# A graph-attention layer's edges in groups of 2048 instead of tiles of 1024, with SyncE's order of loads and stores changed

## The chip, the core and the metric

One core of a Trainium2 chip runs the kernel. The time is device microseconds (us) of one execution. It was taken three times: 4876.2, 4891.12 and 4896.5 us, median 4891.12. One more execution was profiled; it took 4895.69 us.

## The reference, cut to what matters

12,500 nodes with 64 features, 400,000 edges, sorted by their target node dst. All is float32.

```python
h_src, h_dst = nfeats[src], nfeats[dst]
e = leaky_relu(concat([h_src, h_dst, efeats]) @ W_attn + b_attn, 0.01)[:, 0]   # one score an edge
m = concat([h_src, efeats]) @ W_ne                                             # one message an edge
emax = segment_max(e, dst)
ex = exp(e - emax[dst])
z = segment_sum((ex / segment_sum(ex, dst)[dst])[:, None] * m, dst)
out = relu(concat([nfeats, z]) @ W_out)
x = layernorm(nfeats + out)
```

## The kernel before

The edges go through in 391 tiles of 1024 (`ST`), eight on each of 128 partitions. A tile's features lie in one of ten slots of `V` (`RING`): the 64 edge features, loaded by SyncE (`load_ef`), and the 64 features of the source nodes, gathered by POOL with eight indirect DMAs of 128 rows (`gather`, L365). A slot is filled anew when PE has counted up its `v_free` (L902).

Since the edges are sorted, the targets of a tile lie close together. A *window* is 128 consecutive nodes that begin at the tile's first target, one on each partition; they cut through two blocks of 128 nodes, b and b+1, and `half` says which of the two a partition's node is in. Each engine runs an inner loop over the tile's windows (`Fori(0, windows)`), whose number it loads from `trip`. With this input every tile has one window, 391 in all.

What happens in window G, by engine:

- DVE, for the tile two ahead: the product of `V` with the attention weights `wa` (L621) and its sum for each edge, the scores `u` (L625). SyncE stores them to DRAM (L259) and loads them back spread over all partitions as `ubc` (L264), and the tile's targets likewise as `dbc` (L254).
- ACT: `psS`, a huge number wherever an edge's target is not the partition's node, 0 where it is (L498, a Square of `dbc` with a bias).
- DVE: `um` = `ubc` - `psS` and, in the same instruction, its maximum for each node (L735, the *masked maximum*; L735 also stands for the small read of the result). From it and the node's own score come the running bounds (L739, L741) and the new node state (L743).
- ACT: `alpha`, the factor by which older sums must shrink (L502, L505), and the two exponentials `zs` and `zb` of the two branches of the leaky ReLU (L507, L508).
- DVE: `e1` = the greater of both (L694, `weigh`); this is done at the start of the next window.
- PE: transposes `e1` in eight pieces to `psT` (L855), in two halves of four. ACT copies each half to `pT` (L460, `weights_out`). PE multiplies the pieces with `V` into `psG` (L861), each in two passes.
- ACT scales the accumulator rows by `alpha` (L470, `rescale`), and DVE adds `psG` to them (L687, `merge`).

The exponentials, transposes, matmuls and merging of one tile are spread over the following windows: `LAG` = 3 windows lie between a window and its merging, and `psG` has two banks. SyncE's order for each tile is (`step`, L300): wait for the scores and store them, load dst, load the spread scores, load the source indices three tiles ahead (`AHEAD`), wait for the free slot, load the edge features. The loops are written out over ten tiles, one turn of the ring. In the first 70 tiles 49 pairs of node blocks are also transposed and multiplied on the side (`x_pair`, `y_pair`). After the last tile come the division, the second matrix product, the layer norm and the output.

## Time and profile before

| what | value |
|---|---|
| times of three executions | 4876.2, 4891.12, 4896.5 us |
| profiled execution, its time | 4895.69 us |
| its span, first to last instruction | 4893.9 us |
| busy: PE, DVE, ACT, POOL | 2096.0, 2615.8, 2270.5, 3429.4 us |
| granted TensorE clock, mean | 0.650 of full |
| queue q1 (SyncE's loads and stores) | 519.51 MB, 35.5% of the 16 DMA engines' time |
| queue q0 (POOL's gathers) | 102.60 MB, 12.6% |

Busy is the time in which an engine executes; waiting and an engine's own sequencing are not in it. "idle before" is the gap between an instruction and the one before it on its engine, and the name behind it is what ended that gap: "issue" means that nothing in the profile explains it, "remote" that something outside this core's instructions did, often a DMA. A letter q behind an engine's name is its sequencer. The matmuls' ends are modelled.

### The profile page before, as it was taken

To read this page: it belongs to the slowest core of one execution; us is meant where nothing else is said; L and a number is where in the kernel's file an instruction comes from. 1 tells how busy PE (TensorE), PEld (TensorE's weight loads), DVE (VectorE), ACT (ScalarE), POOL (GpSimd) and SP (SyncE) were. 2 spreads that over 40 slices of the span, in tenths; PEclk is the share of its full clock that TensorE was granted. 3 is DMA by queue.
4 is the path that set the end of the run, shared out by engine and by line. 5 is a ranking of instruction groups with operands and counts; after the bars stand their busy time and mean duration, and the time that the engine had idled before them with its cause. 6 is when DMAs were issued, how large, how long until landed. Compare 5 with 4: busy or idle time off the path is not lost.

```text
span 4893.9 us, 64908 instructions
## 1 busy us (share of the span) xinstructions
PE 2096.0 (43%) x10260; PEld 1948.9 (40%) x10261; DVE 2615.8 (53%) x4868; ACT 2270.5 (46%) x4123; POOL 3429.4 (70%) x3149
## 2 busy tenths in 40 slices
PE   0444444444444344443444444444444444444446
PEld 0434444433334334343433433343333334443436
DVE  5545555554555455554555555555545555555557
ACT  1545555544444444444444444444444445444444
POOL 6677776777777667777777767777677777777751
PEclk8666666666666666666666666666666666666666
DMA  5445444554555445444445444554444544544541
GB/s 113 129 124 142 123 132 128 136 132 129 130 133 137 119 130 134 133 134 130 130 132 139 130 122 127 137 134 130 132 128 130 141 130 129 130 130 131 137 124 52
DMA packets 759572, 628.94 MB, mean 129 GB/s; under 512 B 608412, under 2 KB 608796, under 8 KB 759332
## 3 DMA queue, kind: packets, MB, share of 16 engines
q1 hardware_dynamic: 646164, 519.51, 35.5%
q0 software_dynamic: 100096, 102.60, 12.6%
q10 hardware_dynamic: 13072, 4.80, 0.5%
q14 instruction: 233, 1.91, 0.1%
q8 instruction: 7, 0.11, 0.0%
HBM read 621.58 MB, written 4.81 MB: 128 GB/s over the span
## 4 chain that ended last, share of the span: by engine, by line
issue 27%; another core or an unknown queue 23%; DVE 20%; DVEq 13%; ACT 11%; ACTq 5%; PE 2%; POOL 0%
DVE u L625 5%; DVE e L694 5%; DVEq L749 3%; DVE prod L621 3%; ACT psS L498 2%; DVE acc L687 2%; ACT zs L507 2%; DVEq L716 2%; ACT zb L508 2%; ACTq L512 2%; ACT acc L470 1%; ACT pT L460 1%; DVEq L687 1%; DVE bounds L739 1%
## 5 line engine op out<-in xcount | busy, mean ns | idle before, releaser
L365 POOL DMA_INDIRECT V<-in_x_dram,srcs x3128 | 3404.1, 1088 | 1343.3 <-issue 907.5
L855 PE MATMUL psT<-ident,e 128*128 128x128 f32 x3136 | 824.4, 414 | 2739.2 <-DVE e L694 1642.7
L855 PEld LDWEIGHTS psT<-ident,e 128*128 128x128 f32 x3136 | 599.5, 217 | 2882.1 <-DVE e L694 1726.6
L861 PE MATMUL psG<-V,pT 128*128 x6288 | 1364.1, 390 | 0.0
L861 PEld LDWEIGHTS psG<-V,pT 128*128 128x128 f32 x6288 | 1314.5, 307 | 0.0
L460 ACT COPY pT<-psT 128x512 f32<-128x512 f32 x785 | 451.8, 576 | 1372.7 <-remote 1316.1
L621 DVE TENSOR_TENSOR prod<-V,wa 128x1024 f32<-128x1024 f32 x391 | 479.5, 1226 | 563.3 <-issue 563.2
L694 DVE TENSOR_TENSOR e<-zb,zs 128x1024 f32<-128x1024 f32 x392 | 480.4, 1226 | 491.2 <-remote 427.3
L735 DVE CUSTOM_DVE_ANT_0 um<-ubc,psS 128x1024 f32<-128x1024 f32 x391 | 477.3, 1221 | 129.8 <-ACT psS L498 99.3
L625 DVE TENSOR_REDUCE u<-prod 128x8 f32<-128x1024 f32 x391 | 477.0, 1220 | 51.1 <-issue 18.2
L508 ACT ACTIVATE zb<-um,ebias 128x1024 f32<-128x1024 f32 x391 | 442.9, 1133 | 0.0
L498 ACT ACTIVATE psS<-dbc,nbias 128x1024 f32<-128x1024 int32 x391 | 436.9, 1118 | 12.7
L507 ACT ACTIVATE zs<-um,ebias 128x1024 f32<-128x1024 f32 x391 | 442.8, 1132 | 0.0
L502 ACT ACTIVATE ebias<-wnode,nn 128x3 f32<-128x3 f32 x391 | 115.3, 295 | 703.2 <-DVE nn L741 455.0
L687 DVE SCALAR_TENSOR_TENSOR acc<-psG,half,acc x788 | 242.5, 348 | 340.2 <-issue 188.9
L726 DVE TENSOR_SCALAR wnode<-node,half 128x3 f32 x391 | 91.2, 233 | 565.1 <-issue 348.6
L470 ACT ACTIVATE acc<-acc,alpha x788 | 273.3, 397 | 1.3 <-DVE acc L687 1.1
L496 ACT ACTIVATE nbias<-nidbias,wshift 128x1 f32 x391 | 114.9, 294 | 121.7 <-issue 120.0
L505 ACT ACTIVATE alpha<-half,ebias x391 | 115.6, 296 | 108.7 <-issue 61.7
L743 DVE SCALAR_TENSOR_TENSOR node<-keep,nn,node (+1 forms) x391 | 87.0, 223 | 73.5 <-DVE nn L741 38.6
L902 PE MATMUL psR<-ident 128*32 128x128 f32 x390 | 122.9, 315 | 0.0
L739 DVE SCALAR_TENSOR_TENSOR bounds<-slopes,cmax,wnode 128x3 f32<-128x3 f32 x391 | 87.0, 223 | 15.1 <-DVE cmax L735 0.5
(96 smaller groups left out, 620.9 us busy)
## 6 DMA issues: line engine op xcount, KB each, us to landing
ubc<-scores SPq DMA_DIRECT2D x391, 512.0 KB
dbc<-in_dst_dram SPq DMA_DIRECT2D x390, 512.0 KB
V<-in_edge_attr_dram SPq DMA_DIRECT2D x390, 256.0 KB
V<-in_x_dram,srcs POOLq DMA_INDIRECT x3128
scores<-u SPq DMA_DIRECT2D x391, 4.0 KB
srcs<-in_src_dram SPq DMA_DIRECT2D x390, 4.0 KB
out_dram<-y SPq DMA_DIRECT2D x12, 256.0 KB
xt<-in_x_dram ACTq DMA_DIRECT2D x6, 448.0 KB
```

Source lines behind the costliest of these rows:

```text
L365: nc.gpsimd.indirect_dma_start(V[0:n, s, j, 0:F], None, x[:, :], bass.IndirectOffsetOnAxis(ap=srcs[0:n, s, j:j + 1], axis=0)).then_inc(h_i ...
L460: nc.scalar.copy(pT[:, i, :], psT[:, i, :]).then_inc(pt[i], 1)
L498: nc.scalar.activation(psS[:, :], dbc[:, s % 2, :], ACT.Square, bias=nbias[:, 0:1], scale=FAR).then_inc(sq_done, 1)
L507: nc.scalar.activation(zs[:, :], um[:, :], ACT.Exp, bias=ebias[:, 1:2], scale=SLOPE)
L508: nc.scalar.activation(zb[:, :], um[:, :], ACT.Exp, bias=ebias[:, 0:1]).then_inc(e_done, 1)
L621: return nc.vector.tensor_tensor(prod[:, :].rearrange("p (j k f) -> p j k f", k=2, f=F), V[:, s, :, 0:2 * F].rearrange("p j (k f) -> p j k ...
L625: return nc.vector.tensor_reduce(u[:, i, :], prod[:, :].rearrange("p (j f) -> p j f", f=2 * F), AX, ALU.add)
L687: last = nc.vector.scalar_tensor_tensor(row, psG[:, bass.ds(bk, 1), 0:AW].rearrange("p a f -> p (a f)"), half[:, bass.ds(tb, 1), i], row, ...
L694: nc.vector.tensor_tensor(e1[:, :], zb[:, :], zs[:, :], ALU.max).then_inc(mx_done, 1)
L735: nc.vector.tensor_tensor_reduce(out=um[:, :], in0=ubc[:, r, :], in1=psS[:, :], scale=1.0, scalar=-3e38, op0=ALU.subtract, op1=ALU.max, ac ...
L855: last = nc.tensor.transpose(psT[:, i, j * P:(j + 1) * P], e1[:, :].rearrange("q (p j) -> q j p", j=J)[:, 4 * i + j, :], ident[:, :])
L861: last = nc.tensor.matmul(psG[:, bass.ds(bk, 1), 0:AW].rearrange("p a f -> p (a f)"), pT[:, i, j * P:(j + 1) * P], V[:, bass.ds(sv, 1), 4 ...
```

## The change

Two consecutive tiles are now one *group* of 2048 edges: 195 groups and a last one with one tile. A window is gone through once for a group. By the input's targets 192 groups have one window and the last four full ones have two, 200 in all.

- There is one `dbc` and one `ubc` place for each half of a group (h = 0, 1), and both halves go through the one `psS` in turn: square and masked maximum of half 0, then of half 1.
- The leaky ReLU is taken before the exponential. ACT writes `SLOPE` * `um` plus a bias to `psS`, DVE puts the greater of this and of `um` plus a bias into `um` (`low_done`, `lr_done`), half by half. Then one exponential for each half gives `e1`. `zb`, `zs` and L694 are gone.
- ACT's order in a window: nbias, square, square, scaled copy, scaled copy, dif, alpha, rescale, two copies of 128x1024 from `psT` to `pT`, two exponentials.
- PE's order in a window: the 16 matmuls of the group before, then the 16 transposes of this one. `psG` has one bank, `LAG` is 2. The slots of the group before are freed by PE's sequencer once those matmuls are done; the small transpose of L902 is gone.
- The weights of the product lie in PSUM (`wa_v` in `psM`). The node pairs share this PSUM tile, and the product waits for them (`y_ready`), and they for it (`prod_done`).
- SyncE adds up the numbers of windows and waits for `um_done[1]`, the second masked maximum of a group's last window; then it loads the next group's two dst and two spread scores. Behind these it stores the scores of the group after that, loads indices two groups ahead and the edge features. `scores` and `u` have four places instead of two.
- The loops of DVE and SyncE are written out over two turns of the ring.

```diff
-LAG = 3
-BEHIND = 2
-AHEAD = 3
+LAG = 2
+AHEAD = 4
...
+        psT = ps("psT", [P, 2, ST])
+        psG = ps("psG", [P, 512])
         psM = ps("psM", [P, 512])
-        wa_v = wa[:, :].rearrange("p (k f) -> p k f", f=F)[:, 0:3:2, :]
-        xT_y = psM[:, 0:P]
-        y_out = psM[:, P:2 * P]
+        wa_v = psM[:, 0:2 * F].rearrange("p (k f) -> p k f", f=F)
+        xT_y = psM[:, P:2 * P]
+        y_out = psM[:, 2 * P:3 * P]
...
+            def group_read(q):
+                count = sp.value_load(trip[0:1, bass.ds(2 * q + 1, 1)], min_val=1, max_val=NB)
+                sp.reg_add(read, read, count)
+                sp.wait_ge(um_done[1], sp.snap(read))
+            def pair(turn, i, q, odd, stored, last):
+                group_read(q - 2)
+                for h in range(2):
+                    load_dst(2 * q - 2 + h, h)
+                    spread_scores(stored, h, 2 - 2 * odd + h)
+                for h in range(2):
+                    store_scores(2 * q + h, 2 * odd + h)
...
+                for h in range(2):
+                    sp.wait_ge(v_free[2 * i + h], turn + (1 if i == RING // 2 - 1 else 0))
+                    load_ef(RING * turn + 2 * i + h, 2 * i + h)
...
                 windows = act.snap(count, min_val=1, max_val=NB)
-                if ahead:
-                    act.wait_ge(d_in[s % 2], 16 * (RING // 2 * k + s // 2) + 16)
-                else:
-                    act.wait_ge(d_in[s % 2], 16 * (t // 2) + 32)
+                act.wait_ge(d_in[0], arrived[0])
+                act.wait_ge(d_in[1], arrived[1])
...
+                    nc.scalar.activation(psS[:, :], dbc[:, 0, :], ACT.Square, bias=nbias[:, 0:1], scale=FAR).then_inc(sq_done[0], 1)
+                    act.wait_ge(um_done[0], G)
+                    nc.scalar.activation(psS[:, :], dbc[:, 1, :], ACT.Square, bias=nbias[:, 0:1], scale=FAR).then_inc(sq_done[1], 1)
+                    act.wait_ge(wn1, G)
+                    act.wait_ge(um_done[1], G)
+                    nc.scalar.activation(psS[:, :], um[:, 0:ST], ACT.Identity, bias=wnode[:, 4:5], scale=SLOPE).then_inc(low_done[0], 1)
+                    act.wait_ge(lr_done[0], G)
+                    nc.scalar.activation(psS[:, :], um[:, ST:DT], ACT.Identity, bias=wnode[:, 4:5], scale=SLOPE).then_inc(low_done[1], 1)
+                    act.wait_ge(nn_done, G)
+                    nc.scalar.activation(dif[:, :], wnode[:, 2:3], ACT.Identity, bias=nn[:, 0:1], scale=-1.0).then_inc(dif_done, 1)
...
+                    nc.scalar.activation(alpha[:, bass.ds(act.snap(slots[0], min_val=0, max_val=LAG), 1), :].rearrange("p a k -> p (a k)"),
+                                         half[:, bass.ds(q, 1), :].rearrange("p a k -> p (a k)"), ACT.Exp, scale=dif[:, 0:1])
+                    rescale(G)
+                    weights_out(G, 0)
                     weights_out(G, 1)
...
-                    act.wait_ge(nn_done, G)
-                    nc.scalar.activation(ebias[:, :], wnode[:, :], ACT.Identity, bias=nn[:, 0:1], scale=-1.0).then_inc(ebias_done, 1)
...
-                    nc.scalar.activation(zs[:, :], um[:, :], ACT.Exp, bias=ebias[:, 1:2], scale=SLOPE)
-                    nc.scalar.activation(zb[:, :], um[:, :], ACT.Exp, bias=ebias[:, 0:1]).then_inc(e_done, 1)
-                    weights_out(G, 0)
+                    for i in range(2):
+                        act.wait_ge(lr_done[i], G)
+                        nc.scalar.activation(e1[:, i * ST:(i + 1) * ST], um[:, i * ST:(i + 1) * ST], ACT.Exp, bias=nn[:, 0:1]).then_inc(e_done[i], 1)
...
-            def weigh(G):
-                dve.wait_ge(e_done, G)
-                dve.wait_ge(tr[1], G)
-                nc.vector.tensor_tensor(e1[:, :], zb[:, :], zs[:, :], ALU.max).then_inc(mx_done, 1)
...
+                dve.wait_ge(ef_in[s], 16 * turn + 16)
+                dve.wait_ge(h_in[s], 16 * J * turn + 16 * J)
+                if y_steps is not None:
+                    dve.wait_ge(y_ready, y_steps + 1)
+                edge_product(s).then_inc(prod_done, 1)
...
+                    dve.wait_ge(u_in[0], 16 * q + 16)
                     dve.wait_ge(node_set, G)
-                    dve.wait_ge(u_in[r], scored)
-                    dve.wait_ge(e_done, G)
+                    dve.wait_ge(e_done[1], G)
...
-                    weigh(G)
+                    dve.wait_ge(lowf_in, 16)
+                    dve.wait_ge(e_done[0], G)
+                    dve.wait_ge(sq_done[0], G)
+                    nc.vector.tensor_tensor_reduce(out=um[:, 0:ST], in0=ubc[:, 0, :], in1=psS[:, :], scale=1.0, scalar=-3e38,
+                                                   op0=ALU.subtract, op1=ALU.max, accum_out=cmax[:, 0:1]).then_inc(um_done[0], 1)
                     dve.wait_ge(wn0, G)
+                    if left >= 1:
+                        dve.wait_ge(u_in[1], 16 * q + 16)
                     nc.vector.scalar_tensor_tensor(wnode[:, :], node[:, bass.ds(b + 1, 1), :].rearrange("p a k -> p (a k)"), half[:, ts, 1], wnode[:, :],
                                                    ALU.mult, ALU.add).then_inc(wn1, 1)
...
+                    dve.wait_ge(acc_cleared, 2)
+                    dve.wait_ge(um_done[0], G)
+                    dve.wait_ge(sq_done[1], G)
+                    nc.vector.tensor_tensor_reduce(out=um[:, ST:DT], in0=ubc[:, 1, :], in1=psS[:, :], scale=1.0, scalar=-3e38,
+                                                   op0=ALU.subtract, op1=ALU.max, accum_out=cmax[:, 1:2]).then_inc(um_done[1], 1)
+                    dve.wait_ge(um_done[1], G)
+                    nc.vector.tensor_tensor(cm[:, :], cmax[:, 0:1], cmax[:, 1:2], ALU.max).then_inc(cm_done, 1)
...
+                    nc.vector.scalar_tensor_tensor(bounds[:, :], slopes[:, :], cm[:, 0:1], wnode[:, 0:3], ALU.mult, ALU.add).then_inc(bounds_done, 1)
...
+                    for h in range(2):
+                        dve.wait_ge(low_done[h], G)
+                        nc.vector.scalar_tensor_tensor(um[:, h * ST:(h + 1) * ST], um[:, h * ST:(h + 1) * ST], wnode[:, 3:4], psS[:, :],
+                                                       ALU.add, ALU.max).then_inc(lr_done[h], 1)
                     merge(G)
                     pass_on()
...
-                    dve.wait_ge(ef_in[s2], 16 * k2 + 16)
-                    dve.wait_ge(h_in[s2], 16 * J * k2 + 16 * J)
-                    edge_product(s2).then_inc(prod_done, 1)
-                    dve.wait_ge(u_out, 16 * t + 16)
-                    dve.wait_ge(prod_done, t + 1)
-                    edge_score(r).then_inc(u_done, 1)
-                    dve.wait_ge(u_done, t + 3)
...
+                sv = pe.snap(slot[1], min_val=0, max_val=RING - 2)
+                pe.wait_ge(pt[0], G)
+                pe.wait_ge(merged, G + 1)
+                multiply(0, sv)
+                pe.wait_ge(pt[1], G)
+                multiply(1, sv)
                 if turns:
-                    pe.wait_ge(mx_done, G)
-                    pe.wait_ge(pt[0], G)
-                    turn(0)
-                if multiplies:
-                    pe.wait_ge(pt[0], G)
-                    pe.wait_ge(merged, G)
-                    multiply(0, sv, bk)
-                pe.wait_ge(pt[1], G)
-                if turns:
-                    turn(1)
-                if multiplies:
-                    multiply(1, sv, bk)
+                    for i in range(2):
+                        pe.wait_ge(e_done[i], G + 1)
+                        turn(i)
...
-                    nc.tensor.transpose(psR[0:32, 0:P], ident[:, 0:32], ident[:, :]).then_inc(v_free[(s - BEHIND) % RING], 1)
-                    pe.load(coming, trip[0:1, bass.ds(2 * t + 3, 1)])
+                    pe.load(coming, trip[0:1, bass.ds(2 * q + 3, 1)])
+                    pe.wait_ge(agg_done, pe.snap(g))
+                    for h in range(2):
+                        pe.sem_inc(v_free[(2 * i - 2 + h) % RING], 1)
```

The instructions of SyncE in the steady state, before: one tile. `trip` holds the numbers of windows, `u_done` counts DVE's sums, `v_free` PE's releases.

```order
L259 DMA scores<-u 128x8 [waits u_done]
L254 DMA dbc<-in_dst_dram 128x1024
L263 ISA
L264 DMA ubc<-scores 128x1024 [waits u_out]
L248 ISA [waits h_in1]
L248 DMA srcs<-in_src_dram 128x8
L251 ISA [waits v_free8]
L251 DMA V<-in_edge_attr_dram 128x8x64
```

And after: one group.

```order
L306 TENSOR_LOAD trip
L306 ISA x2
L307 ISA
L256 DMA dbc<-in_dst_dram 128x1024 [waits um1_done]
L266 DMA ubc<-scores 128x1024 [waits u_out0]
L256 DMA dbc<-in_dst_dram 128x1024
L266 DMA ubc<-scores 128x1024 [waits u_out1]
L261 DMA scores<-u 128x8 [waits u_done] x2
L250 DMA srcs<-in_src_dram 128x8 [waits h_in4]
L250 DMA srcs<-in_src_dram 128x8 [waits h_in5]
L253 DMA V<-in_edge_attr_dram 128x8x64 [waits v_free0]
L253 DMA V<-in_edge_attr_dram 128x8x64 [waits v_free1]
```

The stores of scores moved from ahead of the loads of dst to behind them; ahead of these stands a load of `trip` and the wait for `um1_done`; the loads of indices and edge features stay last.

ACT before, the second half of a window, from its rescaling of `acc` on; `zs` and `zb` are the exponentials, `tr0` counts the transposes of a first half.

```order
L470 ACTIVATE acc<-acc,alpha 128x129
L502 ACTIVATE ebias<-wnode,nn 128x3 [waits nn_done]
L505 ISA [waits ebias_done,lowf_in]
L505 REGISTER_ALU
L505 ACTIVATE alpha<-half,ebias 128x2
L507 ACTIVATE zs<-um,ebias 128x1024
L508 ACTIVATE zb<-um,ebias 128x1024
L460 COPY pT<-psT 128x512 [waits agg_half,tr0]
```

And after, from the first square of a window on; `um0_done` and `um1_done` count the masked maxima, `lr0_done` the first maximum with the scaled copy.

```order
L525 ACTIVATE psS<-dbc,nbias 128x1024 [waits nbias_done]
L527 ACTIVATE psS<-dbc,nbias 128x1024 [waits um0_done]
L530 ACTIVATE psS<-um,wnode 128x1024 [waits um1_done,wn1]
L532 ACTIVATE psS<-um,wnode 128x1024 [waits lr0_done]
L534 ACTIVATE dif<-wnode,nn 128x1 [waits nn_done]
L537 ISA [waits dif_done,lowf_in]
L537 REGISTER_ALU
L537 ACTIVATE alpha<-half,dif 128x2
L494 ISA
```

Here stand four passes through `psS` in a row (L525 to L532), of which the last three wait for DVE. The rest of that window on ACT, in which `e` is the exponential that PE transposes:

```order
L500 ISA [waits merged,lowf_in]
L500 ACTIVATE acc<-acc,alpha 128x129
L500 ISA
L500 REGISTER_ALU
L500 ACTIVATE acc<-acc,alpha 128x129
L490 COPY pT<-psT 128x1024 [waits agg_half,tr0]
L490 COPY pT<-psT 128x1024 [waits agg_done,tr1]
L544 ACTIVATE e<-um,nn 128x1024 [waits lr0_done]
L544 ACTIVATE e<-um,nn 128x1024 [waits lr1_done]
```

The copies from `psT` to `pT` moved ahead of the exponentials and stand behind the four passes.

## Rows read from the trace of the kernel before

**Rows 1.** The page: the span; queue q1, packets, MB, share; POOL's costliest group.

```profile
span 4893.9 us, 64908 instructions
...
q1 hardware_dynamic: 646164, 519.51, 35.5%
...
L365 POOL DMA_INDIRECT V<-in_x_dram,srcs x3128 | 3404.1, 1088 | 1343.3 <-issue 907.5
```

**Rows 2.** Line L365 alone: ns min/median/max; idle us and times by what ended it.

```profile
L365 POOL DMA_INDIRECT V<-in_x_dram,srcs x3128: 892/946/2022, 4.4 to 4748.2; - x196
...
  issue: 907.5, 2950
```

**Rows 3.** Timeline of POOL, two gathers: start us, us, what.

```profile
2499.66 2.01 POOL L365 DMA_INDIRECT V<-in_x_dram,srcs  x1 [0.30 <-issue]
...
2580.57 0.94 POOL L365 DMA_INDIRECT V<-in_x_dram,srcs  x1 [0.30 <-issue]
```

**Rows 4.** Timeline of DVE beside these two gathers.

```profile
2499.64 1.22 DVE L694 TENSOR_TENSOR e<-zb,zs 128x1024 f32<-128x1024 f32 x1
...
2580.22 1.22 DVE L735 CUSTOM_DVE_ANT_0 um<-ubc,psS 128x1024 f32<-128x1024 f32 x1 [1.90 <-ACT psS L498]
```

**Rows 5.** Timeline of DVE, one undisturbed window.

```profile
2539.88 1.22 DVE L735 CUSTOM_DVE_ANT_0 um<-ubc,psS 128x1024 f32<-128x1024 f32 x1
...
2542.23 0.61 DVE L687 SCALAR_TENSOR_TENSOR acc<-psG,half,acc  x2 [0.27 <-issue]
2543.92 1.23 DVE L621 TENSOR_TENSOR prod<-V,wa 128x1024 f32<-128x1024 f32 x1 [1.08 <-issue]
2545.18 1.22 DVE L625 TENSOR_REDUCE u<-prod 128x8 f32<-128x1024 f32 x1
2547.28 0.23 DVE L726 TENSOR_SCALAR wnode<-node,half 128x3 f32 x1 [0.88 <-issue]
...
2548.77 1.22 DVE L735 CUSTOM_DVE_ANT_0 um<-ubc,psS 128x1024 f32<-128x1024 f32 x1
```

**Rows 6.** Timeline of ACT in the same window.

```profile
2541.59 0.30 ACT L502 ACTIVATE ebias<-wnode,nn 128x3 f32<-128x3 f32 x1 [2.86 <-DVE nn L741]
2542.17 0.29 ACT L505 ACTIVATE alpha<-half,ebias  x1 [0.28 <-issue]
...
2543.41 1.13 ACT L508 ACTIVATE zb<-um,ebias 128x1024 f32<-128x1024 f32 x1
2544.45 0.56 ACT L460 COPY pT<-psT 128x512 f32<-128x512 f32 x1
...
2545.24 1.12 ACT L498 ACTIVATE psS<-dbc,nbias 128x1024 f32<-128x1024 int32 x1
...
2547.11 0.69 ACT L470 ACTIVATE acc<-acc,alpha  x2
```

**Rows 7.** Timeline of PE around one stop.

```profile
2562.14 0.27 PE L902 MATMUL psR<-ident 128*32 128x128 f32 x1
2578.25 1.11 PE L855 MATMUL psT<-ident,e 128*128 128x128 f32 x4 [15.84 <-DVE e L694]
2579.16 1.92 PE L861 MATMUL psG<-V,pT 128*128 x8
```

**Rows 8.** Timeline of POOL at the end of the same stop.

```profile
2577.78 1.23 POOL L365 DMA_INDIRECT V<-in_x_dram,srcs  x1 [3.56 <-remote]
```

**Rows 9.** The masked maximum, line L735 alone: all 391, first and last start.

```profile
L735 DVE CUSTOM_DVE_ANT_0 um<-ubc,psS x391: 1220/1221/1223, 72.8 to 4800.5; 128x1024 f32<-128x1024 f32 x196
```

**Rows 10.** 20 us: length, each engine's busy us (instructions), clock, DMA.

```profile
2557.00:2577.00 20.00, 4.70 (x25) 4.42 (x25) 6.07 (x13) 2.79 (x5) 13.26 (x14) 0.62 0.47 141
```

**Rows 11.** Timeline of SyncE's queue: a load of dst and one of spread scores.

```profile
2546.86 0.38 SPq L254 DMA_DIRECT2D dbc<-in_dst_dram  x1
2547.85 0.33 SPq L264 DMA_DIRECT2D ubc<-scores  x1
```

**Rows 12.** Timeline of POOL: the last gather.

```profile
4748.23 0.90 POOL L365 DMA_INDIRECT V<-in_x_dram,srcs  x1 [0.31 <-issue]
```

More of the change, by code:

```diff
@@ L313, in _ @@
+            sp.wait_ge(trip_in, 16)
+            group_read(0)
+            for h in range(2):
+                load_dst(2 + h, h)
+                spread_scores(1, h, 2 + h)
+            for h in range(2):
+                store_scores(4 + h, h)
             for s in range(AHEAD):
@@ L401, in _ @@
         def _(act):
-            full = NT - 1
+            full = NQ - 1
             for c in range(TC):
@@ L759, in _ @@
[L759 to L764 removed]
+                    dve.load(coming, trip[0:1, bass.ds(2 * q + 2, 2)])
+                for h in range(2 if left >= 3 else 1 if left == 2 else 0):
+                    n = 2 * q + 4 + h
+                    s = (2 * i + 4 + h) % RING
+                    turn = k + (1 if 2 * i + 4 >= RING else 0)
+                    score(n, s, turn, y_steps)
+                    dve.wait_ge(u_out[2 * odd + h], 16 * stored)
+                    dve.wait_ge(prod_done, n - 3)
+                    edge_score(2 * odd + h).then_inc(u_done, 1)
+                    dve.wait_ge(u_done, n + 1)
@@ new lines, in _, with turn_of @@
+            LEFT = 9
+            PH = RING // 2
+            def turn_of(kk, c, y_steps):
+                done = 0
+                for i in range(PH):
+                    n = PH * c + i
+                    node_group(2 * kk + c, i, LEFT, n % 2, PH * kk + n // 2 + 1, None if y_steps is None else y_steps + done)
+                    done += Y_STEPS[i]
+            turn_of(0, 0, 0)
+            with dve.Fori(0, (YT - 1) // 2) as kk:
+                for c in range(1, 3):
+                    turn_of(kk, c, YS * (2 * kk + c))
```

374 lines of the change are left out of this document (178 added, 196 removed).

## The prediction, made before the changed kernel was run

> **What bounds the kernel now.** I read the page first. No engine is full: POOL 70% busy, DVE 53%, ACT 46%, and the loading queue q1 takes 35.5% of the 16 DMA engines' time [rows 1]. But the line that POOL lives on, the gathers of L365, has more in it than its busy time. The gathers took 3404.1 us, the gap of sequencing before each another 907.5 us for 2950 of them, 0.308 us each, and only 1343.3 - 907.5 = 435.8 us of POOL's idle time is waiting [rows 1, 2]. So POOL works 4312 us of the 4749 us that it needs to its last gather [rows 12]: it is 91% taken.
>
> Then I looked for what makes a gather long. The median is 946 ns, the mean 1088 [rows 2]. The gather that starts at 2499.66 takes 2.01 us; at 2499.64 DVE begins L694, the maximum of two SBUF tiles, and the gather is done some 0.9 us after it. Another, from 2580.57, lies inside L735, which reads one SBUF tile and PSUM, and takes 0.94 us [rows 3, 4]. L621, the product, reads two SBUF tiles as L694 does, and gathers beside it are long too. The surplus is 3128 x (1088 - 946) ns = 444 us, and I put it down to these two lines.
>
> The Trainium skill, "SBUF — State Buffer", Who interferes with whom, says that a DVE instruction with two SBUF inputs contends with GpSimd instructions that read SBUF, and infers that descriptor generation is not held up by it. Rows 3 and 4 disagree with the inference. By it the 444 us have another cause and stay, and the sum below would be 4979.
>
> A window of 1024 edges that nothing disturbs takes 8.9 us from one masked maximum to the next (2539.88 to 2548.77) [rows 5], while POOL needs 4312 / 391 = 11.0 us for its eight gathers. The mean window takes (4800.5 - 72.8) / 390 = 12.1 us [rows 9]. The clean windows are faster than POOL, and something stops them until POOL has caught up. A stop looks so: PE has issued the whole window by 2562.4 and starts again only at 2578.25 [rows 7]; in the 20 us from 2557 PE, DVE and ACT do the work of one window while POOL works 13.26 us [rows 10]; then POOL waits 3.56 us for a free slot, and with its end at 2577.78 all run again [rows 8]. The slot is freed by the last PE instruction of that window, long issued by then. I read this as: every so often PE's results stay out until POOL pauses; POOL gets up to its ring's limit, pauses about 3 us, and the clean windows start anew. What holds PE's results back the trace doesn't tell. Whatever it is, the time is POOL's work plus its waits plus the end, and I sum it so.
>
> The Trainium skill, "VectorE: DVE Perf Modes", The TRN2 errata, warns that dense semaphore increments from one engine can deadlock another. It may be of this kind; no row shows it, and nothing below uses it.
>
> **The change, part by part.**
>
> *POOL.* The 3128 gathers stay. L694 goes (its maximum becomes a maximum with PSUM), and the product reads its weights from PSUM. If both free POOL, a gather costs 0.946 + 0.308 = 1.254 us, 3922 us in all, 390 fewer [rows 2]; 16 gathers, one group of 2048 edges, cost 20.1. The bounds of one gather are 1.254 and today's 1.396 (4312 / 3128).
>
> *The chain of a group.* Let T be the start of its first masked maximum (1.22 us, and a 0.08 read). ACT's second square overwrites the same PSUM tile, so it can't start before; with a hand-over of about 0.1 each way it lasts to T+2.5 (1.12, [rows 6]), and the second maximum ends at T+3.9. Then ACT's first scaled copy (no row shows it; 1.12 as the square, bounds 1.12 and 1.13 as the exponential L508) and DVE's first maximum with it (bounds 1.22 and 1.23, L735 and L621), T+6.5; the second copy T+7.8, the second maximum T+9.1. The small steps that give the new minimum take 1.1 today, from the masked maximum's end to merge (2541.10 to 2542.23); they get one more (0.2) and hide beside the first copy, to T+5.2. After its second copy ACT does the difference, alpha (0.6 with the gap) and the rescaling (0.70), to T+9.7, and merge follows (0.61), T+10.4. From merge to product is 1.1 (2542.84 to 2543.92), two products and two sums 4 x 1.24 + 0.1 = 5.1, from the last sum to wnode 0.88, and 0.2 to the next masked maximum: T+17.7 [rows 5, 6]. ACT meanwhile: two copies of 1024 (1.12 each, twice the 0.56 of 512; bounds 1.12 and 1.18), two exponentials, nbias and square, ready at T+15.6. So a clean group takes 17.7 us, against 2 x 8.9 = 17.8 for two windows: the half as many handshakes are paid back by a chain with four passes through one PSUM tile. Bounds, with each of the seven handshakes 0.1 either way and the copies' bounds: 17.0 to 18.5. All lie below POOL's 20.1.
>
> *PE.* 16 transposes and 32 matmul passes in one go: at the 1.11 us of four and 1.92 of eight [rows 7] 4.4 + 7.7 = 12.1 us; it starts at the first copy's end, T+10.8, and needs the results back on ACT at T+27.4 (17.7 + 9.7). 4 us to spare, off the path.
>
> *SyncE.* Today a load of dst is issued right behind the store of a score. Now all four loads of 512 KB wait for the second masked maximum, T+3.9, and the six small or late ones (stores, indices, edge features) stand behind them. q1 moved 519.51 MB in 35.5% of the span, 299 MB per ms [rows 1], so 2.1 MB need 7.0 us alone; issues lie 0.99 us apart [rows 11], so they land about T+13 to T+15. ACT wants them at T+14.3. This cover is thin: each us more goes on the 17.7, of which POOL hides 2.3. Behind the waiting SyncE stand the scores of the group after next, needed a group later, and the edge features, for which DVE waits a group and a half later. Hidden.
>
> *Windows.* By the inputs' dst each of the 391 tiles spans under 128 nodes; of the 196 groups the last four full ones span more and take two windows. A window without scoring costs 17.7 - 6.2 = 11.5 us.
>
> *POOL's waits.* The ring still holds ten tiles, but the tiles in work are six of them, so the lead is smaller. If the stops come as often by time and each ends with a pause of about 3 us, the waits stay near 436 us. Bounds: 0, and 830 us if a group takes what two windows take now (24.2 us x 196 = 4743 = 3922 + about 830). I take 436, the row's own number, plus 12 for the release behind group 191's second window.
>
> *The end.* Before, 51 us pass from POOL's last gather to the last masked maximum (4749.1 to 4800.5) and 93.4 from there [rows 9, 12]. Now the last gathers end about 10 us into group 192; what is left of it (19), group 193 (27) and 194 (23) make 69, and with 93 it is 162.
>
> *The 49 node pairs* that are turned and multiplied in the first 70 tiles are now done where the product waits for them; POOL's 2.3 us a group hide them. Without that cover it is 49 x about 1 us.
>
> *Sum:* 2 (start) + 3922 + 436 + 12 + 162 = 4534 us of span, and 1.8 around it (4895.7 - 4893.9): **4535 us**, against 4895.7 for the profiled execution and 4891.1 in the median, which are the same within 0.1%.
>
> **The rivals.**
>
> *The stops go.* PE's results no longer get stuck, since a group has fewer instructions and handshakes. Then POOL hardly waits: 4535 - 436 = 4100. For it: clean windows already run faster than POOL. Against: stops are far apart in program position and follow whenever POOL runs for long, and POOL will run more densely.
>
> *PSUM operands don't free POOL for the product.* Then only L694's share of the 444 us goes, about half: 4535 + 220 = 4755. If the surplus has another cause than either line, as in the sentence on the SBUF page, all of it stays: 4979. Against both stands the gather beside L735 [rows 3, 4].
>
> *The stops cost what they cost, per edge.* A group takes 24.2 us, the waits grow to 830: 4535 + 394 = 4930, no change. For it: if a limit on some traffic that doesn't change (bytes, gathers) sets today's 12.1 us. Against: two windows in a row run at 8.9.
>
> *The release is late (slower).* Today all that PE does in a window is issued at once, so the pause is over when its results come: 3.56 us. Now PE frees a group's slots after the matmuls of the next window; a stop that hits in the transposes behind them leaves POOL to finish another group and then to wait for two copies and 32 passes, 2.2 + 7.7 + 3 = about 12 us. If a third of some 150 waits are of this kind, the waits are 100 x 2.9 + 50 x 12 = 890, 4535 + 454 = 4990; if half, 1120 and 5220. It decides from waits of 797 us on, 5.3 us in the mean of 150. For it: a third of PE's work in a group are transposes.
>
> **How the numbers follow.** Forecast (waits 250 to 600) 0.42; stops go 0.13; product not freed 0.09, another cause 0.02; same cost per edge 0.14; late release 0.20. The forecast's own range is 4350 to 4700. From the cases I leave out 0.1 below 4200 and 0.1 above 5020. What can be told from no change is 0.5%, 25 us. Faster is the first three and a little of the fourth: 0.69; within 0.5% 0.09; slower 0.22.
>
> **What the profile after would show.** The gathers' mean near 950 ns, with none of 2 us: the port. POOL's idle time beside the 0.3 us gaps: near 450 is the forecast, near 0 the first rival, near 830 or more the third or fourth; single waits of 10 us and more are the fourth. The DVE timeline: 17 to 18.5 us from one first masked maximum to the next where nothing disturbs, 1.1 to 1.3 us between the paired steps. ACT's first square waiting for a DMA would show that the four loads come too late. Wrong altogether would be a clean group above 20 us, for then POOL is not what bounds it.

## The result and the profile after

The changed kernel took 5007.14 us in the median of four executions (4995.41 to 5014.39), the kernel before 4890.84: a ratio of 1.024, 95% interval 1.0209 to 1.0271. It is slower; 4535 was forecast.

These rows answer to [rows 1, 2]. The page after has the span and POOL's costliest group (busy us and mean ns, then idle before):

```profile
span 4993.5 us, 52597 instructions
...
L395 POOL DMA_INDIRECT V<-in_x_dram,srcs x3128 | 2953.7, 944 | 1860.5 <-issue 938.7
```

The gathers' line alone has min/median/max in ns, and what ended POOL's idle time (us, times):

```profile
L395 POOL DMA_INDIRECT V<-in_x_dram,srcs x3128: 892/944/1763, 4.6 to 4814.9; - x196
...
  PEq L950: 917.4, 163
```

The gathers became as short as forecast, 3404.1 down to 2953.7 us. But POOL now waits 917.4 us for PE's release (L950), 163 times and 5.6 us in the mean, where it waited 436 us in all. The waits grew by 486 us, from 436 to 922 (4.4 us of these are for indices), and ate the gain of 450.

What is waited for shows in one group. PE reports the end of its work by counting up a semaphore; this is called its *report* here. The end of a matmul is modelled in these profiles, the time of a report is recorded. First PE, from the matmuls (L915) whose end frees two slots:

```profile
2914.37 6.69 PE L915 MATMUL psG<-V,pT 128*128 x32 [5.07 <-issue]
2920.90 1.93 PE L909 MATMUL psT<-ident,e 128*128 128x128 f32 x15
2925.39 0.27 PE L909 MATMUL psT<-ident,e 128*128 128x128 f32 x1 [2.57 <-issue]
```

POOL in the same time:

```profile
2929.39 0.95 POOL L395 DMA_INDIRECT V<-in_x_dram,srcs  x1 [0.31 <-issue]
2934.14 0.94 POOL L395 DMA_INDIRECT V<-in_x_dram,srcs  x1 [3.81 <-PEq L950]
```

And SyncE's queue:

```profile
2933.54 1.66 SPq L253 DMA_DIRECT2D V<-in_edge_attr_dram  x2
2936.22 0.33 SPq L256 DMA_DIRECT2D dbc<-in_dst_dram  x1
```

The matmuls are over at 2921.1. Their report (the count of `agg_done`) comes 12 us later, at 2933.3, 2.9 us after POOL's last gather ended (2930.3). It is the stop of [rows 7, 8]. Over the whole trace the report comes 7.5 us after the last matmul in the mean of the 191 groups for which it is recorded, and over 1 us late in 148 of them. The release by PE's sequencer (L950), recorded for all, comes 8.1 us late in the mean. Late reports are not new: in the kernel before they came 5.4 us late in the mean, and over 1 us late for 291 of 372 tiles. New is that POOL waits longer for them. SyncE stands behind the same release: the second masked maximum was over at 2927.9, yet dst is loaded from 2936.2 on.

Something else is slow in the stops. In that of [rows 7, 8], from 2559 to 2576, SyncE's own steps (register moves and issues of loads) begin mostly 1.4 us apart, where 0.1 to 0.4 us is usual. Of one kind of step, the register move ahead of a load of dst, the profile after has (ns min/median/max):

```profile
L256 SPq MOVE dbc<-in_dst_dram x360: 2/29/1396, 126.5 to 4498.4; - x180
```

Such a step waits for nobody. Of SyncE's 1809 register steps without a wait between 200 and 3600 us, 348 took over 0.5 us, 86% of these while a report of PE was out. So did 75 of DVE's 1686, all of them then, and 94 of ACT's 1556, 23% of them then. So a stop is more than a late report of PE. The reports of DVE and ACT aren't late where the trace has them (90% within 0.01 us), but it has only half of them.

### The profile page after: what moved, and what is told of

The parts are those of the page before. It is cut to its first block, busy times and chain, and to the rows that moved or that the text cites. A ratio compares the mean times of both kernels' runs of the same rounds, so it can differ in the third digit from the quotient of the medians.

```text
span 4993.5 us, 52597 instructions
## 1 busy us (share of the span) xinstructions
PE 1739.6 (35%) x10078; PEld 1656.2 (33%) x10079; DVE 2413.6 (48%) x3752; ACT 2039.5 (41%) x2811; POOL 2979.2 (60%) x3149
## 4 chain that ended last, share of the span: by engine, by line
issue 37%; another core or an unknown queue 16%; ACT 15%; DVE 14%; PE 7%; DVEq 4%; ACTq 3%; DMA 1%; PEld 1%; SPq 0%; PEldq 0%; POOL 0%
PE psG L915 4%; ACT psS L532 3%; DVE um L786 3%; DVE um L772 3%; ACT e L544 3%; DVE prod L661 3%; ACT psS L527 2%; ACT psS L530 2%; ACT psS L525 2%; DVE u L665 2%; PE psT L909 1%; ACT acc L500 1%; DVEq L792 1%; PEld psG L915 1%
## 5 line engine op out<-in xcount | busy, mean ns | idle before, releaser
L395 POOL DMA_INDIRECT V<-in_x_dram,srcs x3128 | 2953.7, 944 | 1860.5 <-issue 938.7
L915 PE MATMUL psG<-V,pT 128*128 x6432 | 1241.9, 378 | 2875.4 <-ACT pT L490 1451.8
L915 PEld LDWEIGHTS psG<-V,pT 128*128 128x128 f32 x6432 | 1193.6, 290 | 2934.7 <-issue 2934.6
L490 ACT COPY pT<-psT 128x1024 f32<-128x1024 f32 x402 | 387.6, 1006 | 740.4 <-remote 657.4
L786 DVE SCALAR_TENSOR_TENSOR um<-um,wnode,psS 128x1024 f32<-128x1024 f32 x400 | 511.9, 1280 | 273.5 <-ACT psS L532 154.3
L661 DVE TENSOR_TENSOR prod<-V,psM 128x1024 f32<-128x1024 f32 x391 | 477.3, 1221 | 191.3 <-issue 184.8
L909 PE MATMUL psT<-ident,e 128*128 128x128 f32 x3200 | 440.6, 285 | 261.2 <-issue 261.0
L909 PEld LDWEIGHTS psT<-ident,e 128*128 128x128 f32 x3200 | 401.5, 193 | 273.2 <-issue 272.9
L544 ACT ACTIVATE e<-um,nn 128x1024 f32<-128x1024 f32 x400 | 438.4, 1148 | 0.0
L530 ACT ACTIVATE psS<-um,wnode 128x1024 f32<-128x1024 f32 x200 | 223.5, 1117 | 308.4 <-DVE cmax L772 175.5
L532 ACT ACTIVATE psS<-um,wnode 128x1024 f32<-128x1024 f32 x200 | 223.4, 1117 | 273.4 <-DVE um L786 192.1
L525 ACT ACTIVATE psS<-dbc,nbias 128x1024 f32<-128x1024 int32 x200 | 223.5, 1117 | 6.7
L722 DVE SCALAR_TENSOR_TENSOR acc<-psG,half,acc 128x129 f32 x404 | 125.0, 347 | 137.7 <-remote 65.7
L500 ACT ACTIVATE acc<-acc,alpha x404 | 140.8, 395 | 0.4 <-issue 0.3
```

Of the source, the lines that this page charges most:

```text
L395: nc.gpsimd.indirect_dma_start(V[0:n, s, j, 0:F], None, x[:, :], bass.IndirectOffsetOnAxis(ap=srcs[0:n, s, j:j + 1], axis=0)).then_inc(h_i ...
L490: nc.scalar.copy(pT[:, i, :], psT[:, i, :]).then_inc(pt[i], 1)
L525: nc.scalar.activation(psS[:, :], dbc[:, 0, :], ACT.Square, bias=nbias[:, 0:1], scale=FAR).then_inc(sq_done[0], 1)
L532: nc.scalar.activation(psS[:, :], um[:, ST:DT], ACT.Identity, bias=wnode[:, 4:5], scale=SLOPE).then_inc(low_done[1], 1)
L544: nc.scalar.activation(e1[:, i * ST:(i + 1) * ST], um[:, i * ST:(i + 1) * ST], ACT.Exp, bias=nn[:, 0:1]).then_inc(e_done[i], 1)
L661: return nc.vector.tensor_tensor(prod[:, :].rearrange("p (j k f) -> p j k f", k=2, f=F), V[:, s, :, 0:2 * F].rearrange("p j (k f) -> p j k ...
```

## The experiments

Each was timed beside the kernel before on the same chip, and ratios are to that. The kernel before took 4885 to 4891 us beside e1 to e8, e17 and e18, on three chips, and 4954 beside e15 and e16, on the chip of e1 to e4. Beside e9 to e12 it took 4465 us and beside e13 and e14 4489, on two other chips. The chips were not chosen; e13 takes up what this means. T is the start of a group's first masked maximum, as in the prediction.

**e1. SyncE's order.** The features are loaded one pair later, so their wait no longer stands between a group's indices and the next group's dst.

```diff
                     spread_scores(stored, h, 2 - 2 * odd + h)
+                features(turn, i - 1)
...
-                for h in range(2):
-                    sp.wait_ge(v_free[2 * i + h], turn + (1 if i == RING // 2 - 1 else 0))
-                    load_ef(RING * turn + 2 * i + h, 2 * i + h)
```

> The changed kernel, but SyncE loads the edge features of a group one pair later, behind the next group's dst and scores and not ahead of them; their wait for the slots' release then no longer stands ahead of the wait for the second masked maximum. Loop theory (POOL works 20 us a group and then has to rest some 4 us until PE's results come out, and everything else is slaved to that): the loads of dst leave at T+4 instead of T+12, but POOL's waits stay near 920 us and the time within 1% of 5007 us. SyncE theory (the late loads set the group's period): a group goes from 24.2 to 18 to 20.5 us, POOL's waits fall under 300 us, the time to 4300 to 4450 us.

4996.95 us, ratio 1.0238 (1.0217 to 1.026). The line of the gathers alone:

```profile
  PEq L957: 917.1, 163
```

The waits are the same to 0.3 us. The place of the features in SyncE's order is not the cause. SyncE's own waiting for the release went from 1077.1 to 26.1 us, yet the median start of the loads came forward only from about T+10.5 to T+7.6: SyncE's steps are slow here too. From 3001.4 to 3011.2 it waits for nobody and takes seven steps of 0.7 us, 1.4 apart, to its load of dst.

**e2. The port alone undone:** the product reads `wa` from SBUF.

```diff
-                                               wa_v.unsqueeze(1).broadcast_to((P, J, 2, F)), ALU.mult)
+                                               wa[:, :].rearrange("p (k f) -> p k f", f=F)[:, 0:3:2, :].unsqueeze(1).broadcast_to((P, J, 2, F)), ALU.mult)
```

> The changed kernel, but the product reads its weights from SBUF again, so it has two SBUF inputs. Port theory: gathers beside it become long (up to 2 us), the mean goes from 0.944 to about 1.00 us, POOL's work grows by 150 to 200 us, and as POOL sets the pace the time becomes 5150 to 5200 us. If POOL's work is not what sets the pace (SyncE theory), the gathers get longer, POOL's waits shorter by as much, and the time stays within 0.5%. If the surplus had another cause than these lines, the gathers' mean stays 0.944.

4915.16 us, ratio 1.0058 (1.0039 to 1.0077): 92 us faster than the change, though every theory had it slower or equal. The gathers did get longer, 944 to 972 ns in the mean:

```profile
L395 POOL DMA_INDIRECT V<-in_x_dram,srcs x3128: 892/944/1988, 4.9 to 4733.6; - x196
...
  PEq L950: 752.6, 140
```

With the gaps, POOL works 84 us more; it waits 165 us less. The port theory holds for the gathers' length and fails for the time: shorter gathers cost more in waits than they save.

**e3. POOL rests** after every fourth gather.

```diff
+                    if napping and j in (3, 7) and s in (0, 1, 2, 3, 4, 5, 6, 7, 8, 9):
+                        nc.gpsimd.memset(nap[:, :], 0.0).then_inc(nap_done, 1)
+                        pool.wait_ge(nap_done, pool.snap(naps))
+                        pool.reg_add(naps, naps, 1)
```

> The changed kernel, but POOL rests after every four gathers: it clears a small tile and waits for that, some 1 us each, four rests a group. If PE's results come out only in a rest of 3 us or more, nothing comes out earlier, the rests add to the waits, and a group takes 28 us, 5700 to 5900 us in all. If short rests let them out too, the release of the slots comes during the group's gathers, POOL's waits for it nearly vanish (under 200 us instead of 920), and the time is between 4800 and 5050 us. SyncE theory: release and loads come earlier, as in the second case.

4983.03 us, ratio 1.0203 (1.0186 to 1.022). 760 rests were added and the time did not grow:

```profile
  issue: 1247.1, 2943
  POOL nap L403: 159.4, 183
  PEq L959: 33.1, 1
```

917 us of waits became 33, and these are one wait at 140 us, near the start. A pause of about 1.4 us between two gathers, after each fourth, is enough: the report of the matmuls now comes 0.1 us late in the mean. SyncE's loads leave at T+4.3 in the mean and land at T+13.3, and its register steps are fast again (11 of 1808 over 0.5 us). So late reports and slow steps of SyncE go together.

**e4. Half the gathers** from the ring's second turn on; the other source features stay those of the first turn, and the counts that are waited for are halved to match.

```diff
-                    gather(s, P)
+                    gather(s, P, J // 2)
```

> The changed kernel, but only four of the eight gathers of a tile are made from the ring's second turn on (half of the source features stay old). Loop theory: POOL works 10 us a group, the stops need POOL's long runs and go, and the clean group is left: 17 to 18 us, 3500 to 3700 us in all. If PE's results are held back by something else that is unchanged (the 128 GB/s of loads, the code), groups keep 22 us and more, 4500 us and more in all.

3729.44 us, 3727.2 the span. From one first masked maximum to the next it takes 3537 / 199 = 17.8 us in the mean by this row, and 16.8 in the median:

```profile
L762 DVE CUSTOM_DVE_ANT_0 um<-ubc,psS x200: 1206/1221/1223, 88.9 to 3625.9; 128x1024 f32<-128x1024 f32 x100
```

With the same loads and the same work on the other engines the reports are prompt (0.03 us late in the mean). POOL makes eight gathers in a row and then waits 8.2 us in the mean (1566.9 us, 191 times). So it is POOL's long runs of gathers that make the stops.

**e5, e6, e7. Fewer and shorter rests:** after every 8th gather; after the 8th of 16 only; after every 4th, with 128x2 cleared in place of 128x512. Against e3, in this order:

```diff
-                    if napping and j in (3, 7) and s in (0, 1, 2, 3, 4, 5, 6, 7, 8, 9):
+                    if napping and j in (7,) and s in (0, 1, 2, 3, 4, 5, 6, 7, 8, 9):
...
-                    if napping and j in (3, 7) and s in (0, 1, 2, 3, 4, 5, 6, 7, 8, 9):
+                    if napping and j in (7,) and s in (0, 2, 4, 6, 8):
...
-        nap = sb("nap", [P, 512])
+        nap = sb("nap", [P, 2])
```

> The changed kernel, but POOL rests after every eight gathers (clears 128x512, waits for it; with four such rests a group each added 1.07 us and POOL's waits for a release were gone). Rest theory (PE's results come out in any short rest of POOL, and half a group of gathers is not yet too long): POOL's waits for a release stay under 100 us, 380 rests less cost 405 us less than the four-rest version, 4983 - 405 = 4580 us, 4540 to 4680. Count theory (what helped was a rest every four gathers, stops form within eight): waits come back, 4750 to 4950 us.

> As the two-rest version, but one rest a group, after its eighth gather; after the sixteenth none. Rest theory: the matmuls end at about the middle of POOL's run, and a rest in a fixed place in the run may miss them; if it catches them, 4583 - 190 = 4380 us; if it misses them, POOL waits at the end of a group as without rests and the time is 4900 to 5050 us. I take some of both, 4450 to 4750 us.

> As the four-rest version, but each rest clears only 128x2, so it is shorter, I take 0.5 to 0.7 us added and not 1.07. If the length of the rest doesn't matter, waits stay near 30 us and the time is 4983 minus 760 x 0.4 to 0.5, 4620 to 4700 us. If PE's results need about a microsecond of rest, POOL's waits come back, to 300 us and more, and the time is 4850 us and more.

| rests a group | us | ratio | rests cost | waits for release |
|---|---|---|---|---|
| none (the change) | 5007 | 1.024 | 0 | 917 |
| 1 | 4995 | 1.0228 (1.0204 to 1.0252) | 202 | 699 |
| 2 | 4884 | 0.9998 (0.9979 to 1.0017) | 367 | 419 |
| 4 | 4983 | 1.0203 (1.0186 to 1.022) | 881 | 33 |
| 4 short | 4822 | 0.987 (0.9849 to 0.989) | 460 | 276 |

Rests cost: clearing, plus idle time ended by it or by nothing, less the 938.7 of the change. For two rests the count theory was right, 4580 us was far off: within eight gathers the reports get stuck again. One rest missed the 4450 to 4750 us that I took and fell where a rest was expected to miss the matmuls. Four short ones fell between their two cases: the waits came back, but less than expected. A microsecond of rests takes away 1.0 to 1.1 us of waits with one or four long rests and 1.4 with two or with four short ones. Four short ones gave the first version faster than the kernel before where there are stops, by 1.3%.

**e8. The kernel before with a rest** after every 16th gather.

```diff
+                    if napping and j in (7,) and s in (0, 2, 4, 6, 8):
+                        nc.gpsimd.memset(nap[:, :], 0.0).then_inc(nap_done, 1)
...
```

> The kernel before, with one such rest after every sixteenth gather. Rest theory: the stops are the same in it; 196 rests cost 210 us and take POOL's 436 us of waits down to 100 or less: 4891 - 336 + 210 = 4765 us, 4700 to 4850. If the rests only add to the waits, 5100 us.

4908.0 us, ratio 1.0042 (1.0028 to 1.0056). A miss by 140 us: POOL's idle time beside the gaps fell only from 436 to 348 us. That the long gathers already rest POOL in this kernel would fit e2, but no run shows it.

**e9, e10. Parts of the change in the kernel before:** the release by PE's sequencer; and with it the weights in PSUM.

```diff
-                    nc.tensor.transpose(psR[0:32, 0:P], ident[:, 0:32], ident[:, :]).then_inc(v_free[(s - BEHIND) % RING], 1)
                     pe.load(coming, trip[0:1, bass.ds(2 * t + 3, 1)])
+                    pe.wait_ge(agg_done, pe.snap(g))
+                    pe.sem_inc(v_free[(s - BEHIND) % RING], 1)
...
-        wa_v = wa[:, :].rearrange("p (k f) -> p k f", f=F)[:, 0:3:2, :]
+        wa_v = psR[:, P:2 * P].rearrange("p (k f) -> p k f", f=F)
```

> The kernel before with one part of the change: a tile's slot is freed by PE's sequencer, which waits until the matmuls are reported done, and not by a small transpose behind them. If the way of the release is what costs (PE's queue now stands while a report is out, so the next tile's transposes start late), POOL's waits rise from 436 us to 600 and more, and the time to 5000 us and more. If it is only the report itself that is late, in both ways alike, no change: 4870 to 4915 us.

> As the last one, and the product reads its weights from PSUM. In both theories the gathers beside the product become short, the mean goes from 1.088 to about 1.03 us, POOL's work falls by some 187 us. My prediction's rule (time is POOL's work plus waits that stay): 187 us faster than the last one. Rest theory (a long gather is a rest too, and its loss is given back in waits): within 1% of the last one, slower rather than faster.

On this chip the kernel before took 4464.78 us. e9: 4475.63 us, ratio 1.0021 (1.0003 to 1.004). e10: 4163.85, ratio 0.9325 (0.9312 to 0.9338). In e9 POOL never waits for anything but its first indices:

```profile
  issue: 953.0, 3127
  DMA srcs<-in_src_dram: 2.6, 1
```

There is no stop in it. From e9 to e10 the gathers get 322 us shorter (3417 to 3095, where 187 were expected) and the time 312 us: here all is gained, as the prediction's rule said. Neither run says what the release by PE's sequencer does where there are stops, which is what e9 was made for.

**e11, e12,** on that chip too: e7 with e1's order; and two short rests a group, after the 12th and the 16th gather.

> The four short rests (4822 us), and SyncE's loads of edge features one pair later, as in the first experiment. With the short rests POOL still waits 276 us for releases and SyncE's loads of dst leave at T+10 in the mean. If the loads' place in the queue matters once POOL's waits are few, the time falls to 4700 to 4780 us; if everything waits for the same late report, 4800 to 4840 us.

> Two short rests a group, both in its second half (after the twelfth and the sixteenth gather). The matmuls whose report is awaited end when POOL is some 15 us into its run of 20, so only rests behind that can help. If the place counts, waits stay near the 276 us of four short rests, and the time is 4822 - 215 = 4610, up to 4750 us. If the number of gathers in a row counts, two rests do less than four: waits of 450 us and more, 4800 to 4900 us.

4647.84 us, ratio 1.0408 (1.0393 to 1.0422), and 4397.47, ratio 0.985 (0.9836 to 0.9864). Without stops a rest is only a cost, so neither tells what it was made for.

**e13. The changed kernel again.**

> The changed kernel once more, beside runs of the kernel before on the same chip. On one chip the kernel before took 4465 us and POOL never waited in the kernels run there; on the others it took 4888 us and they had the stops. If the chip of this call is of the first kind: rest theory says no stops, so POOL's work and the end alone are left, 3922 + 2 + 162 and the two-window groups 12, 4100 us, within 60, a ratio of 0.92 to the kernel before. If it is of the second kind: 5007 us again, ratio 1.02. A rival for the first kind: the late loads of dst and the late release are the change's own fault, then it is slower than the kernel before there too, 4550 us or more.

It fell on another chip without stops: 4154.38 us against 4489.32, ratio 0.9253 (0.9227 to 0.9278), within the 4100 ± 60 of the rest theory. The gathers' line:

```profile
L395 POOL DMA_INDIRECT V<-in_x_dram,srcs x3128: 896/944/1702, 4.8 to 3976.7; - x196
...
  PEq L950: 70.7, 37
```

PE and SyncE in one group of it, and SyncE's register move over the whole run:

```profile
3064.32 5.60 PE L915 MATMUL psG<-V,pT 128*128 x32 [10.64 <-ACT pT L490]
3069.76 1.93 PE L909 MATMUL psT<-ident,e 128*128 128x128 f32 x16
```

```profile
3058.24 0.34 SPq L256 DMA_DIRECT2D dbc<-in_dst_dram  x1
```

```profile
L256 SPq MOVE dbc<-in_dst_dram x360: 29/29/37, 112.3 to 3718.8; - x180
```

The same program, with the same gathers of 944 ns, is 7.5% faster than the kernel before here. The report follows the last matmul by 0.01 us in the mean of the whole trace, against 7.5 us; the release is at 3070.4, 0.5 us behind the last matmul; dst leaves 4.0 us after the masked maximum of 3054.2. No such register step of SyncE, DVE or ACT takes over 0.5 us, and the trace has 99% of DVE's and ACT's reports. So the release, the order of loads and the group's chain are sound where nothing is held up, and what makes the change slow elsewhere comes with the stops.

**e14, e15. e10 again,** on e13's chip, and on a chip with stops.

> The kernel before with release by PE's sequencer and weights in PSUM, once more. On a chip with stops: rest theory says that the shorter gathers are given back in waits, ratio 0.99 to 1.02; the rule that waits stay says 4888 - 310 = 4580 us, 0.94. On a chip without: 0.93 as before.

> The kernel before with release by PE's sequencer and weights in PSUM; so far it ran twice where nothing is held up, 0.93 of the kernel before. If this chip has the stops (kernel before near 4890 us): rest theory, the 310 us of shorter gathers are given back in waits, ratio 0.99 to 1.02; the rule that waits stay, 0.94. If it has none, 0.93 again.

4172.27 us, ratio 0.9288 (0.9259 to 0.9317), and 4999.57 us against 4954.0, ratio 1.0093 (1.0074 to 1.0112). In the latter the gathers are shorter than in the kernel before (997 ns against 1088) and the waits long:

```profile
L366 POOL DMA_INDIRECT V<-in_x_dram,srcs x3128 | 3117.2, 997 | 1732.6 <-issue 913.5 <-PEq L907 782.6 <-DMA srcs<-in_src_dram 36.5
```

So the gain is given back in windows of 1024 edges too: 287 us less of gathers, 383 us more of waits. The run has two edits, though. The release by PE's sequencer was not timed alone on a chip with stops, so its share isn't known; e2, whose one edit is the gathers' length, is the cleaner run.

**e16. e12 again,** on e15's chip.

> The changed kernel with two short rests in a group's second half; on a chip without stops it took 0.985 of the kernel before. If this chip has the stops: place theory (rests behind the end of the matmuls do all the work of four) 4610 to 4750 us; count theory 4800 to 4900 us.

5044.04 us, ratio 1.0173 (1.015 to 1.0197), with 804 us of waits. The place theory (4610 to 4750 us) fell. The count theory had waits of 450 us and more right and its 4800 to 4900 us wrong. Two short rests do much less than the two long, evenly spaced ones of e5 (419 us); whether the twelve gathers without a rest or the rests' length makes the difference was not tested.

**e17, e18. Gathers of 64 rows; and four short rests again,** both on a third chip with stops (kernel before 4890.56). In e17 the source features of half the edges stay old.

```diff
-                    gather(s, P)
+                    gather(s, P // 2)
```

> The changed kernel, but from the ring's second turn on each gather brings 64 rows and not 128 (half of the source features stay old); the number of gathers stays. On a chip with stops: if it is the number of gather instructions that holds PE's reports back, POOL's waits stay and the time is that of the change less what a gather of 64 rows is shorter (I don't know that, 0 to 0.4 us each, 5007 down to 3900), with reports still out for 10 us and more; if it is the rows, reports come at once and a group takes 17 to 18 us, or POOL's 16 gathers if those are longer. On a chip without stops only POOL's shorter gathers show, 3600 to 4150 us.

> The changed kernel with four short rests a group, 0.987 of the kernel before on a chip with stops. There: the same again, 0.98 to 0.99. On a chip without stops the rests are only a cost, 760 x 0.55 = 420 us on 4154, 4570 us, 1.02.

e17: 4967.19 us, ratio 1.016 (1.0143 to 1.0177):

```profile
L395 POOL DMA_INDIRECT V<-in_x_dram,srcs x3128: 894/902/1696, 4.8 to 4780.6; - x196
...
  PEq L950: 879.1, 144
```

With half the rows a gather takes 902 ns in place of 944 (medians), and the reports are out no shorter (9.5 us in the mean, against 7.5). With e4, which has half the rows by half the gathers and no stops, it is the number of gather instructions that matters, not their rows. e18: 4825.9 us, ratio 0.987 (0.9854 to 0.9887), as e7.

## Why the prediction was wrong

**The failed step is "POOL's waits".** It took 436 us over from the kernel before, as if each stop were worth one pause of 3 us however POOL runs. On the chips that have stops the pauses behave like a rest that POOL owes for gathers made close together: shorter gathers mean more waiting. e2 (POOL works 84 us more, waits 165 less) shows it, e3 (waits gone for 881 us of rests) shows it from the other side, and e15 fits (ratio 1.009, against 0.93 for the same kernel without stops), with the release as a second edit. The waits were 922 us and not 436 + 12. The gathers with their gaps took 2953.7 + 938.7 = 3892 where 3922 was forecast, and 178 us and not 162 passed after the last one (4815.8 to 4993.5). With 1.6 us at the start this is the 4993.5 of the span.

One number says it more shortly. From start to last gather, POOL made one gather per 1.518 us in the kernel before (4749.1 / 3128), 1.540 in the change, 1.514 in e2, 1.541 in e3, 1.551 in e15, 1.529 in e17, 1.500 in e5 and 1.48 in e7 and e18. Without stops it was 1.398 in e9, 1.296 in e10, 1.272 in e13. Where there are stops the pace stays within 5% whatever one does to the gathers. In e3 alone it is POOL's own work and rests that set it, since it hardly waits.

**The rivals.** "The stops cost what they cost, per edge" (0.14) named this, a limit on some traffic that doesn't change, and gave 4930. What doesn't change is the number of gathers (e4, e17). "The release is late" (0.20) was nearest in time (waits 890, 4990), and 30 of the waits are of its kind, 8 to 12 us, but 128 of the 163 are of 3 to 5 us, about one pause for each report, and in e13 POOL waits 70.7 us for a release where reports are prompt. How much of the waiting comes from POOL's smaller lead (the prediction has six of the ring's ten tiles in work) was not tested on a chip with stops. "The stops go" (0.13) foresaw 4100; it is what chips without stops do, 4154. I argued against the per-edge limit with "two windows in a row run at 8.9". That was no argument: 8.9 us is what a window takes after a pause, not what POOL can keep up (11.0 by the prediction's own sum).

**Right:** the mean of a gather ("near 950 ns": 944, and 1.254 us with its gap became 1.244). The clean group, 17.7 us with bounds of 17.0 to 18.5: 17.8 in the mean of e4, though by the median an undisturbed one takes 16.8, below the bounds; what I had too long was the chain up to the copies (first copy forecast to end at T+10.8, it does at T+9.8). PE's 12.1 us for a group were too long too (6.7 and 1.9 for its 32 passes and 16 transposes), off the path. SyncE's four loads, landing forecast for T+13 to T+15: T+13.3 in e3, T+13.8 in e4 and T+14.1 in e13, by the landings that the traces have. "Hidden" for what stands behind them was right only with prompt reports: I didn't price that the features' wait for the release also stands ahead of the *next* group's dst. e1 shows that this cost nothing on top.

**Two readings.** The long gather of [rows 3] ends 0.8 us after L694 (0.9 was said), and the short one doesn't lie quite inside L735 but ends 0.07 us behind it. And the inference that the prediction takes from the Trainium skill, "SBUF — State Buffer", Who interferes with whom, is not refuted by these rows: a gather also reads its indices (`srcs`) from SBUF, and no run here tells that read from the making of descriptors. What they and e2 show is that the gather as a whole gets longer.

**Open:** what holds PE's reports back and slows the steps of SyncE, DVE and ACT while POOL gathers, and whether one is the cause of the other or both have the same; whether the matmuls themselves end late, since their ends are modelled; why three chips (12 of the runs) have it and two (6 runs) don't, and whether it is the chip or something else that differed between the runs.

## What to carry to other kernels

Before a saving on one engine is booked, ask what the waits in the profile are made of. If they follow that engine's own work, the pauses will grow by what the work shrinks. And where an engine's results come late with no work in front of them, look at the sequencers' own steps on the other engines too, and run both kernels on several chips: here one change is worth +2.4% or -7.5%.

## What the runs showed of the hardware

- While POOL made indirect gathers of 128 rows 1.25 us apart, the reports of finished matmuls were late on three of five chips: in the changed kernel by 7.5 us in the mean and up to 17, those of the transposes up to 38. On two chips the delay was 0.01 us with the same gathers.
- Of the 148 reports that were over 1 us late there, 129 came in a pause of POOL, half of these between 2.9 and 3.1 us after the end of its last gather; with gathers of 64 rows (e17) it was 151 of 163, half of them between 3.6 and 3.8 us after it.
- In the same runs single register moves of SyncE took up to 1.4 us; on the two other chips (e13) at most 0.04.
- Pauses of about 1.4 us after every fourth gather let the reports out (0.1 us late in the mean, waits 33 us); pauses after every eighth left waits of 419 us.
- A gather of 64 rows took 902 ns, one of 128 rows 944 (medians).
- With a DVE product of two SBUF inputs beside them the gathers took 972 ns in the mean (e2); with one input in PSUM 944.
